# Attention stages: softmax sums taken from ones beside the values and parted from the results by SBUF transfers; a shorter second mask product

## The reference, cut to what matters

```
scores = q @ k.T * 16 ** -0.5          # 128 x 128, causal
p      = exp(scores - rowmax)          # masked entries give 0
out    = (p @ v) / p.sum(-1)           # 128 x 16
y      = x + concat_heads(out) @ Wo + bo
```

## Time and profile before

| | |
|---|---|
| time, median of 3 runs | 2940.9 us (2937.07 to 2945.79) |
| the profiled execution: its own time | 2936.01 us |
| the profiled execution: span of the trace | 2934.1 us |
| busy share of the span: PE, PE weight load | 94%, 87% |
| busy share of the span: DVE, ACT, POOL | 76%, 63%, 54% |
| attention stages in the trace | about 35 to 577 us and 2182 to 2727 us |
| one pair in the steady part of such a stage | 16.29 us |

### The profile page before, as it was taken

The page is one execution under the profiler, slowest core; times in us unless marked ns, Lnnn a source line. Parts: engine busy times, 40 slices in busy tenths (PEclk is TensorE's granted clock), DMA queues, the critical chain, the costliest instruction groups (busy, mean ns, idle before and its releaser), DMA issues. The chain is left out here.

```text
span 2934.1 us, 79455 instructions
## 1 busy us (share of the span) xinstructions
PE 2769.7 (94%) x26879; PEld 2561.8 (87%) x26880; DVE 2240.0 (76%) x6196; ACT 1861.9 (63%) x6939; POOL 1584.6 (54%) x1816
## 2 busy tenths in 40 slices
PE   6999999899999999999999999999989999999947
PEld 5888888689999999998899999999988888888447
DVE  6988888877777777776877777777768888888735
ACT  5889999755555555555544444444449999998535
POOL 3666666467777777776322222222225666665566
PEclk9999999999999999999999999999999999999979
DMA  6000000010000000000100000000010000000245
GB/s 229 18 20 15 18 15 15 2 64 11 11 11 11 11 11 11 11 11 15 35 12 11 13 13 11 11 11 11 5 48 16 17 16 16 18 17 3 94 153 162
DMA packets 56480, 88.30 MB, mean 30 GB/s; under 512 B 6959, under 2 KB 42800, under 8 KB 55473
## 3 DMA queue, kind: packets, MB, share of 16 engines
q1 hardware_dynamic: 48848, 66.97, 7.4%
q0 software_dynamic: 6528, 16.92, 1.6%
q10 hardware_dynamic: 864, 1.84, 0.2%
HBM read 58.28 MB, written 28.48 MB: 30 GB/s over the span
## 5 line engine op out<-in xcount | busy, mean ns | idle before, releaser
L679 ACT ACTIVATE L_probs<-bank,L_neg_max 128x128 f32<-128x128 f32 x2048 | 718.6, 404 | 115.3 <-DVE L_neg_max L764 110.8
L679 ACT ACTIVATION_READ_ACCUMULATOR L_probs<-bank,L_neg_max 128x1 f32 x2048 | 499.4, 244 | 0.0
L770 DVE COPY L_probsT<-bank 128x512 f32<-128x512 f32 x512 | 341.5, 686 | 107.8 <-PE bank L549 105.7
L1911 ACT ACTIVATE M_inter<-bank 128x512 f32<-128x512 f32 x256 | 153.3, 599 | 386.6 <-PE bank L69 386.6
L67 PE MATMUL bank<-W_hi,M_nT_hi 128*128 128x384 f32 (+1 forms) x1024 | 368.8, 360 | 7.3 <-DVE M_qkv L1496 4.5
L764 DVE TENSOR_REDUCE L_neg_max<-bank 128x4 f32<-128x512 f32 x512 | 327.4, 681 | 31.2 <-PE bank L539 31.1
L68 PE MATMUL bank<-W_hi,M_nT_lo 128*128 128x384 f32 (+1 forms) x1024 | 346.0, 338 | 0.0
L69 PE MATMUL bank<-W_lo,M_nT_hi 128*128 128x384 f32 (+1 forms) x1024 | 345.8, 338 | 0.0
L1978 DVE TENSOR_TENSOR M_inter_lo<-M_inter,M_inter_hi 128x512 fp32r<-128x512 f32 x256 | 184.0, 719 | 177.9 <-ACT M_inter_hi L1912 172.8
L549 PE MATMUL bank<-constants,L_probs 128*128 128x128 f32 x2048 | 303.3, 280 | 12.7 <-ACT L_probs L679 10.5
L67 PE MATMUL bank<-M_nT_hi,W_hi 128*128 128x256 f32 x1024 | 294.2, 287 | 0.0
(11 more groups left out here) (342 smaller groups left out, 9025.9 us busy)
## 6 DMA issues: line engine op xcount, KB each, us to landing
L_ctx_in<-in_ctx SPq DMA_DIRECT2D x64, 256.0 KB, 2.6
M_tile<-M_sorted SPq DMA_DIRECT2D x72, 130.0 KB, 2.6
x_all<-in_x SPq DMA_DIRECT2D x8, 1024.0 KB, 10.1
raw_weights<-in_weights SPq DMA_DIRECT2D x2, 4096.0 KB, 15.2
hs<-M_hs SPq DMA_DIRECT2D x64, 128.0 KB, 1.7
M_hs<-hs SPq DMA_DIRECT2D x31, 256.0 KB, 2.6
raw_weights<-in_weights SPq DMA_DIRECT2D x1, 2048.0 KB, 7.7
M_sorted<-M_fill SPq DMA_DIRECT2D x12, 130.0 KB, 2.7
```

Source lines behind the costliest of these rows:

```text
L679: last = act.activation(probs[:, k % UNITS, i, :], score_bank[u][:, i, :], ACT.Exp, bias=neg_max[:, u, i:i + 1], scale=-1.0, accum_out=sum ...
L770: dve.tensor_copy(probsT[:, k % UNITS], pT_ps[k % UNITS]).then_inc(pT_ready, 1)
L1911: act.activation(inter[:, e % 2], up_bank[e % 2], ACT.Gelu).then_inc(M.inter_ready, 1)
```

## The change

The softmax sum is no longer accumulated by ACT. `v_pad` now holds, for each head, its 16 value columns at even places and ones at the odd places between them. The product of values and probabilities then gives, on alternating partitions of bank 5, a result row and the softmax sum. Since results and sums now stand on different partitions, they have to be brought side by side. ACT copies the whole bank to `o_mixed` (`keep_o`, after the exponentials of unit 1 of a half), SP issues four transfers SBUF to SBUF of 64 partitions x 1 KB each (`rejoin`), the odd partitions into `o_sum`, the even ones into `o_raw`. DVE takes the reciprocal of all of `o_sum`, 128x256, in place, and multiplies (`scale_o`, inside the row maxima, after that of unit 2); POOL multiplies once and forms the rest. `scale_o(n)` and `normalize(n)` run two halves later than the scores of n. Gone are `accum_out`, `invert`, `spread`, `turn_recip` and DVE's `keep_o`; `keep_v` is two instructions for four. In s = 1 `project_o` moves behind the `turn_p` of units 1 and 2. The mask is coded so that the second set of four products covers only the last 50 of 128 keys of each head (4x50 = 200 columns for 512). The orders of weights follow. SP's stream is now unrolled over the pairs, with the load of context p + 3 ahead of the transfers of step p.

```diff
+FULL_GROUPS = 32 - 6
+LATE = 3 * FULL_GROUPS
...
+                def rejoin(n, b):
+                    sp.wait_ge(o_kept, n + 1)
+                    wait(sp, o_ready, n - 1)
+                    for r, tile in ((1, o_sum), (0, o_raw)):
+                        for a in range(2):
+                            mixed = o_mixed[r:P:2, b, KT * a:KT * (a + 1), :].rearrange("p m q -> p (m q)")
+                            sp.dma_start(tile[P // 2 * a:P // 2 * (a + 1), b, :], mixed).then_inc(o_joined[b], 16)
+                def step(p, b):
+                    if more(p, 3):
+                        load(p + 3, 1 - b)
+                    if not is_(p, 0):
+                        rejoin(2 * p - 1, 1)
+                    rejoin(2 * p, 0)
...
+                        pe.matmul(score_bank[u][:, :, LATE:], S.late_q16[at, :],
+                                  S.late_k16[at, LATE:].unsqueeze(1).broadcast_to([32, UH, P - LATE]),
+                                  start=False, stop=True, skip_group_check=True)
...
-                        if exists:
-                            turn_recip(before[0], before[2] // UNITS - 1)
-                        for half in range(2):
-                            if s == 0 and more(p, 1):
-                                project_q(p + 1, half)
-                            if s == 1 and not is_(p, 0):
-                                project_o(p - 1, half)
+                        if s == 0 and more(p, 1):
+                            for m in range(KT):
+                                project_q(p + 1, m)
                         turn_p(p, UNITS * s + 1)
                         turn_p(p, UNITS * s + 2)
                         if s == 0 and more(p, 2):
                             turn_n(p + 2)
+                        if s == 1 and not is_(p, 0):
+                            for half in range(2):
+                                project_o(p - 1, half)
...
                         last = act.activation(probs[:, k % UNITS, i, :], score_bank[u][:, i, :], ACT.Exp,
-                                              bias=neg_max[:, u, i:i + 1], scale=-1.0,
-                                              accum_out=sums[:, s, u // 2, i, u % 2:u % 2 + 1])
+                                              bias=neg_max[:, u, i:i + 1], scale=-1.0)
                     last.then_inc(exp_done, 1)
+                def keep_o(n):
+                    act.wait_ge(pv_done, UNITS * (n + 1))
+                    wait(act, o_joined[n % 2], 64 * (n // 2))
+                    act.activation(o_mixed[:, n % 2].rearrange("p u q -> p (u q)"), S.bank[5], ACT.Copy).then_inc(o_kept, 1)
...
+                def scale_o(n):
+                    b = n % 2
+                    dve.wait_ge(o_joined[b], 64 * (n // 2 + 1))
+                    dve.reciprocal(o_sum[:, b], o_sum[:, b]).then_inc(sum_inverted, 1)
+                    dve.wait_ge(sum_inverted, n + 1)
+                    wait(dve, o_ready, n)
+                    dve.tensor_tensor(o_sb[:], o_raw[:, b], o_sum[:, b], ALU.mult).then_inc(o_scaled, 1)
...
                         for u in range(1, UNITS):
                             row_max(p, UNITS * s + u)
+                            if u == 2 and not is_(p, 0):
+                                scale_o(2 * p + s - 2)
                         keep_p(p, UNITS * s)
-                        if exists:
-                            keep_o(*before)
```

More of the change, by code:

```diff
@@ L93, in constants @@
     causal = k[:, None] <= k[None, :]
[L95 to L100, removed]
+    rows, keys, later = 2.0 ** np.array([75, 24, -27]), np.array([0.0, 2.0 ** -51, 1.0]), 2.0 ** 51
+    hide_q, hide_k = np.zeros((2, P, P)), np.zeros((2, P, P))
+    for n, begin in enumerate(range(0, P, 3)):
+        end = min(begin + 3, P)
         for u in range(UNITS):
-            at = (n // 32, 32 * u + (n if n < 32 else n - 32 + 6))
-            hide_q[at][begin:end], hide_k[at][begin:end], hide_k[at][end:] = rows, keys, later
-        begin = end
+            at = (0, 32 * u + 6 + n) if n < FULL_GROUPS else (1, 32 * u + n - FULL_GROUPS)
+            hide_q[at][begin:end], hide_k[at][begin:end] = rows[:end - begin], keys[:end - begin]
+            hide_k[at][end:] = later
     def thirds(v):
@@ L374, in attention @@
     UP = 2 * UNITS
-    rest_k16 = S.rest_count_k16 if counted else S.rest_k16
+    mask_k16 = S.mask_count_k16 if counted else S.mask_k16
     with ExitStack() as mem:
@@ L450, in _ @@
                     load_x(sp, S, x_dram, 3)
-                    load(2, 0)
+                load(2, 0)
+                if first:
                     load_x(sp, S, x_dram, 4)
                     load_x(sp, S, x_dram, 5)
-                    load(3, 1)
                     load_x(sp, S, x_dram, 6)
@@ L459, in _ @@
                 next_loaded = load_next(sp)
[L460 to L465, removed]
+                pairs(sp, step, True)
+                rejoin(2 * NP - 1, 1)
                 if first:
@@ L521, in score @@
                 def score(p, b, s):
[L523 to L531, removed]
+                    for u in range(UNITS):
+                        at = slice(32 * u, 32 * u + 32)
+                        wait(pe, exp_done, UP * p + UNITS * (s - 1) + u + 1)
+                        if u == 0:
+                            wait(pe, pT_ready, UP * p + UNITS * (s - 1) + 2)
+                        pe.matmul(score_bank[u], S.mask_q16[at, :], mask_k16[at, :].unsqueeze(1).broadcast_to([32, UH, P]),
+                                  start=True, stop=True)
+                    for u in range(UNITS):
+                        at = slice(32 * u, 32 * u + 32)
+                        pe.matmul(score_bank[u][:, :, LATE:], S.late_q16[at, :],
+                                  S.late_k16[at, LATE:].unsqueeze(1).broadcast_to([32, UH, P - LATE]),
+                                  start=False, stop=True, skip_group_check=True)
                     if s == 0:
@@ L561, in times_v @@
                     for i in range(UH):
-                        last = pe.matmul(o_ps[32 * i:32 * (i + 1), 0, m, :], v_pad[:, b, s, e, UH * m + i, :],
+                        last = pe.matmul(o_ps[32 * i:32 * (i + 1), u, :], v_pad[:, b, s, UH * u + i, :],
                                          probsT[:, u, i, :], start=u == 0, stop=True, skip_group_check=True)
                     last.then_inc(pv_done, 1)
[L566 to L571, removed]
                 def step(p, b):
@@ L688, in step @@
                         exps(p, u)
+                        if u == 1 and not is_(p, 0):
+                            keep_o(2 * p - 1)
                     if more(p, 1):
@@ L724, in _ @@
                 pairs(act, step, True)
-                if not first:
+                if first:
+                    keep_o(2 * NP - 1)
+                else:
                     act.activation(S.warm[:], S.one, ACT.Sqrt)
@@ L750, in keep_v @@
                     wait(dve, pv_done, UP * (p - 1))
[L751 to L757, removed]
+                    for s in range(2):
+                        last = dve.tensor_tensor(
+                            v_pad[:, b, s].rearrange("p h (d r) -> p h d r", r=2)[:, :, :, 0],
+                            v_ps[:, s, :].rearrange("p (h d) -> p h d", d=D),
+                            bias.v.rearrange("p (h d) -> p h d", d=D), ALU.add)
                     last.then_inc(v_ready, 1)
@@ L963, in step @@
                     if not is_(p, 0):
-                        normalize(p - 1, 1)
-                    spread(p, 0)
+                        normalize(2 * p - 2)
                     if more(p, 1):
                         split_q(p + 1)
-                    normalize(p, 0)
-                    spread(p, 1)
+                    if not is_(p, 0):
+                        normalize(2 * p - 1)
                     if first and is_(p, 0):
```

87 lines of the change are left out of this document (33 added, 54 removed).

## The result

| | before | changed |
|---|---|---|
| median (4 runs each) | 2942.09 us (2937.07 to 2945.79) | 3126.28 us (3123.31 to 3127.53) |
| ratio to before, 95% interval | | 1.0629 (1.0615 to 1.0642) |
| profiled execution: own time, span | 2936.01, 2934.1 us | 3127.53, 3125.6 us |
| mean granted clock | 0.983 | 0.958 |
| steady pairs, from one residual to the next | 16.29 us | 18.8 to 19.5 us |

The changed kernel is 6.3% slower. The forecast was 3086 us with the range 3035 to 3145, so the time lies in the range and 40 us above the forecast.

A forecast was written before the change was run, and what follows sets the result against it. PE was taken as tightest before, with DVE close behind, and the changed loop as DVE-bound by the reciprocal. 2936 + 118 (pairs) + 7 (layer ends) + 20 (clock) = 3081, runs' median 5 above: 3086 us, range 3035 to 3145.

The forecast's parts named there:

- The reciprocal decides: On DVE, the reciprocal grows from 16 to 256 columns and takes 1.80 us, bounds 0.53 and 2.25.
- The rival with 2.25 us: DVE's reciprocal takes its upper bound of 2.25 us, +56 us, about 3142 us in total; chance 0.08.
- The new pair: Steady attention loop: s = 0 8.85 us, s = 1 9.35, pair 18.20 against 16.29; 62 x 1.91 = +118 us.
- The clock: Clock falls after PE's new 2.3 us pause in s = 1, 1.15 us each; 20 us taken, bounds 0 and 71.
- the rival with a fall in every pair: The clock falls in every pair: 71 us in place of 20, about 3137 us in total; chance 0.15.
- The first pairs of layer 0: They carry extra statistics on DVE in both kernels and were to change by the same as the other pairs.
- The layers' ends: Way from each layer's last product to its last projection grows: 3.5 us per layer, 7 in all.
- Transfers hidden: SP's four issues per half take 1.6 us, landing 1.7 (bounds 1.7 and 2.6); slack over 2.5 us hides them.
- PE's saving: On PE, `turn_recip` gone saves 0.22 us per half, the shorter mask 0.13; 0.70 per pair, at most 45 us.
- The turning point: Reciprocal length on DVE that decides between faster and slower: 0.85 us, near 110 columns.
- DVE as the bound: In steady windows DVE becomes the busiest engine, over 90%, with PE down to 85 to 88%.
- ACT: 16 exponentials without sum reads take about 4.0 us for 5.5; ACT eased about 0.9 us per half, costed at nothing.

The follow-up runs named there:

- the pause filled: Changed kernel with eight unread bf16 products of 128x512 put on PE between the transposes of units 1 and 2 in s = 1; ratio to before 1.0427, pair 18.17 us.
- the short mask: Kernel before with only the new mask coding and the 200-column second mask products; ratio to before 0.9972, pair 16.19 us.
- The run with 0.94 us: Changed kernel with the reciprocal over only the first 128 of 256 columns, the other sums used uninverted; ratio to before 1.0091, pair 16.57 us.

## Why the prediction was right, and where it was short

- **The reciprocal decides: right.** Forecast 1.80 us, measured 1.74. Taking it out takes out the whole loss (0.9949), putting it alone into the kernel before brings most of it (1.0499). The rival with 2.25 us fell, and with it the price taken from the Trainium skill (VectorE: DVE Perf Modes, the walkthrough): the page gives a repeat count of 8, which at one clock of 0.96 GHz per repeat would by estimate be 8.3 ns per column. These runs show 6.3 from 128 to 256 columns, so the count can't be read as a time in that way.
- **The new pair: right.** s = 0 was forecast at 8.85 us and is 8.83, s = 1 at 9.35 and is 9.35, the pair at 18.20 and is 18.18 where the clock stays at full. PE's pause was put at 2.3 us and is 2.0. So 62 x 1.91 = 118 us stands, nearly: with the pause filled, the pairs are 18.17.
- **The clock: right in kind, the term mis-sized.** I took 20 us between 0 and 71; measured, 59 from the difference of the ratios, 59 from the count of the falls, and 58 from two traces (the stretches from the first residual to the last but two are 564.41 and 555.47 us in the two layers of the changed kernel, 534.76 and 526.73 with the pause filled). This one term is nearly all of the forecast's error, and the rival with a fall in every pair, at 3137 us and a chance of 0.15, came nearer to the measured 3126 than the forecast did. Two steps in it were off. "A bit over a quarter" of the pairs was a guess that rested on the one place in layer 0 where nothing fell; it was about two pairs of three (38 of 60), and five of the first six of layer 0. And 1.15 us per fall was read from the scores alone, while the low stretch covers output projection, mask and scores: 1.56 us in the pair shown.
- **The first pairs of layer 0: short.** "Change by the same" did not hold: the first ones go from 16.9 to 20.3 us, +3.4. The run with the filled pause has 18.8 there: +1.9 as forecast, and 1.5 of clock.
- **The layers' ends: forecast 7, a few us more.** The last two intervals of a layer grow by 9.6 and 7.5 us; less two pairs' 1.9 each, that leaves 5.8 and 3.7, where 3.5 each were taken. How much of it is the clock was not parted: with the pause filled the last two intervals are no shorter.
- **Closing the sum.** The profiled executions differ by 191.5 us. From the first to the last residual of the two layers it is 95.7 + 91.1 = 186.8; the other 4.7 lie ahead of the first residual and between and behind the layers, for which I had no term. The last two intervals of each layer are 17.1 of the 186.8. The other 58 intervals grow by 169.7, of which 111.3 stand there with the pause filled too (1.92 each, forecast 1.91) and 58.4 are the clock. The profiled execution is 46 us above the 3081 of the sum: the clock's term is 38 of it, the ends 2.5, and the 4.7 had no term.
- **Transfers hidden: right, with a price misread.** Four issues take 2.4 us of SP's time in the timeline (one group of two takes 1.10, the other 1.24), not the 1.6 scaled from the context loads, and they land in 2.0 to 2.1 us. The slack took it, and took twice as much.
- **PE's saving: mask over-rated.** 0.13 us per half was forecast, 0.11 is at the place shown, and 0.10 per pair arrives. In s = 0 PE saves as much (from the mask to the next transposes 1.42 for 1.54), but the half is 8.29 us long in both kernels: DVE has no pause in its last 4.7 us (410.01 to 414.70 with the short mask), so DVE sets its end. Without the reciprocal's price, the change saves 0.29 us per pair (16.29 to 16.00) of the 0.70 that was the most it could.
- **The turning point** was put at 0.85 us per reciprocal. The run with 0.94 us gives a pair of 16.57. From there to 1.74 us the pair grows by 1.61 us for 0.80, 2.0 per us; going back at that slope, 16.29 is met at 0.80 us, and by a straight line to 16.00 at 0.28 us it is met at 0.62. So it lies between 0.6 and 0.8, a little lower than I put it.
- **DVE as the bound: half of it.** I forecast DVE over 90% busy in steady windows and the busiest; it is 87 in the changed kernel, as much as PE, and 92 with the pause filled. The falls stretch PE's part, in which DVE waits. And even at full clock DVE is busy for only 16.53 of 18.18 us. "DVE-bound" holds for s = 0; in s = 1 it is the order, PE's chain behind a copy that stands behind the reciprocal, as the layout of the pair had it.
- **ACT: a price misread, without effect.** Eight exponentials without reads take 2.34 us (at 402.94), so 16 take some 4.6 us for the 4.0 forecast. It was costed at nothing, and PE waits for ACT only 7.8 us in the whole trace.

## What to carry to other kernels

A sum that is spread before it is inverted is inverted many times over: here 16 different values per token took 0.24 us as 16 columns and 1.74 us as 256. Where the engine that inverts is nearly full, invert first and spread afterwards.

An engine that is not the bound can still be the one that decides: DVE had 2.1 us to spare in a window of 16.2; it got rid of some 1.8 (two copies, two small reciprocals, part of `keep_v`) and took on 4.2. By the amount alone, 14.06 and 2.4 more, the pair would be some 16.5 us by estimate; it is 18.2, because in s = 1 PE stands still behind the reciprocal and DVE then behind PE. Count what the second-fullest engine gets before counting what the fullest one saves, and lay out who waits behind it. Where a new pause of some 2 us appears on PE, price the clock in most pairs, over all the work that follows the pause.

## What the runs showed of the hardware that I had not expected

- The clock falls not in PE's pause but when work is taken up behind it: at 1.00 from 424 to 426 us with PE idle, at 0.50 from 428 to 430 with PE full. A pause of 2.0 us in every pair brought it in two pairs of three; single pauses of 1.2 us (half a reciprocal) left the steady windows at 1.00. But four shorter ones, of 0.15 to 0.86 us and 2.3 us in all within some 4 us, brought it in every steady pair (the reciprocal as the half's last step), so the length of one pause is not all that counts. Eight products for nothing in the pause saved 59 us.
- Each further column of a reciprocal costs nearly the same, 5.2 to 6.5 ns: 164 ns for 1 column, 242 for 16, 527 for 60, 941 for 128, 1743 for 256, where a copy of 256 columns takes 0.28 us and a product 0.43.
- POOL's product of two tiles of 256 columns takes 0.97 us where its other operations of that width take 0.73 (line 948: 727 ns). It starts when the reciprocal ends, as DVE's own product of the same tiles does; whether that is the reason was not tested.
